# Expert loop of an attention-and-experts kernel: where the second bias is added, when GpSimd adds it, and how the routing arithmetic is spread

## The reference

```
x = x + xattn(layernorm(x), ctx)                # 16 heads, then relu(out W1 + b1) W2 + b2
logits = x @ Wg;  e = argmax(logits)            # 8 experts, one for each token
h   = gelu((xhat * s_e + b_e) @ W1_e + b1_e)    # 512 -> 128
x   = x + h @ W2_e + b2_e                       # 128 -> 512
```

## Time and profile before

| | |
|---|---|
| median of three runs | 1582.67 us |
| the profiled execution's own time | 1584.45 us |
| its span, first to last instruction | 1582.6 us |
| TensorE matmul busy | 1515.4 us, 96% |
| VectorE busy | 1037.9 us, 66% |
| ScalarE busy | 713.1 us, 45% |
| GpSimd busy | 441.9 us, 28% |
| mean granted TensorE clock | 0.987 |

### The profile page before, as it was taken

The page is one execution under the profiler, slowest core; times in us unless marked ns, Lnnn a source line. Parts: engine busy times, 40 slices in busy tenths (PEclk is TensorE's granted clock), DMA queues, the critical chain, the costliest instruction groups (busy, mean ns, idle before and its releaser), DMA issues.

```text
span 1582.6 us, 24339 instructions
## 1 busy us (share of the span) xinstructions
PE 1515.4 (96%) x7988; PEld 1254.6 (79%) x7988; DVE 1037.9 (66%) x2496; ACT 713.1 (45%) x2015; POOL 441.9 (28%) x312
## 2 busy tenths in 40 slices
PE   6799999999999999999999999999999999997998
PEld 3688788787878787878787788878787878776886
DVE  5756566675758576766666675757575757467776
ACT  2545445353535363635444353535353636333443
POOL 3422122121222222212131122122222222136776
PEclk8899999999999999999999999999999999999999
DMA  9200101112020202020101101010101011548773
GB/s 230 80 28 1 54 1 40 42 31 74 3 86 1 74 14 74 22 75 21 61 27 54 34 23 38 17 54 1 54 1 54 1 54 54 215 153 261 232 226 112
DMA packets 67736, 105.93 MB, mean 67 GB/s; under 512 B 26967, under 2 KB 35432, under 8 KB 66591
## 3 DMA queue, kind: packets, MB, share of 16 engines
q1 hardware_dynamic: 56814, 70.68, 15.9%
q0 software_dynamic: 10800, 33.70, 5.5%
HBM read 59.47 MB, written 46.72 MB: 67 GB/s over the span
## 4 chain that ended last, share of the span: by engine, by line
PE 60%; DVE 23%; DMA 7%; ACT 4%; issue 3%; POOL 2%; DVEq 0%; POOLq 0%; SPq 0%; ACTq 0%
PE bank L1025 13%; PE bank L1050 12%; PE bank L887 11%; PE bank L911 5%; PE bank L1005 5%; DMA region<-rows,pos 4%; DVE actH L994 4%; PE bank L1455 4%; PE bank L1499 4%; DMA rows<-in_x 3%; DVE xn L845 2%; POOL region L1193 2%; ACT actH L988 2%; PE bank L1119 2%; PE bank L1438 2%
## 5 line engine op out<-in xcount | busy, mean ns | idle before, releaser
L1050 PE MATMUL bank<-w,actH 128*128 128x512 f32 x1536 | 373.8, 393 | 4.6 <-DVE actH L1040 4.6
L1025 PE MATMUL bank<-actA,w 128*128 128x512 f32 x1536 | 366.7, 394 | 0.0
L1025 PEld LDWEIGHTS bank<-actA,w 128*128 128x128 f32 x1536 | 286.0, 188 | 62.2
L1050 PEld LDWEIGHTS bank<-w,actH 128*128 128x128 f32 x1536 | 282.4, 188 | 62.9 <-DVE actH L1040 8.6
L970 POOL TENSOR_TENSOR E<-E,rc 128x1232 f32<-128x1232 f32 x64 | 145.0, 2265 | 447.6 <-DVE rc L965 447.6
L1040 DVE TENSOR_TENSOR actH<-htmp,actH 128x512 fp32r<-128x512 f32 x128 | 88.7, 693 | 166.8 <-ACT actH L1036 148.1
L1035 ACT ACTIVATE htmp<-bank,b 128x512 f32<-128x512 f32 x128 | 88.2, 689 | 226.1 <-PE bank L1025 217.4
L887 PE MATMUL bank<-actA,wq 128*128 128x512 f32 x768 | 182.0, 390 | 0.0
L943 ACT ACTIVATE E<-bank,mx 128x77 f32<-128x77 f32 x512 | 157.6, 365 | 45.4 <-DVE mx L920 45.4
L887 PEld LDWEIGHTS bank<-actA,wq 128*128 128x128 f32 x768 | 144.2, 188 | 30.4 <-issue 0.5
L1193 POOL DMA_INDIRECT region<-rows,pos x64 | 63.1, 985 | 373.0 <-DVE pos L1187 333.9
(11 more groups left out here) (165 smaller groups left out, 2063.3 us busy)
## 6 DMA issues: line engine op xcount, KB each, us to landing
rowB<-region SPq DMA_DIRECT2D x71, 258.0 KB
rows<-in_x SPq DMA_DIRECT2D x64, 256.0 KB, 3.5
e_raw<-in_E SPq DMA_DIRECT2D x16, 256.0 KB, 2.7
region<-padrow SPq DMA_DIRECT2D x9, 258.0 KB, 2.6
w_raw<-in_W SPq DMA_DIRECT2D x1, 2048.0 KB, 10.3
w_raw<-in_W SPq DMA_DIRECT2D x2, 1024.0 KB, 8.5
e_parts<-e_high SPq DMA_DIRECT2D x8, 256.0 KB, 2.0
e_parts<-e_low SPq DMA_DIRECT2D x8, 256.0 KB, 2.3
```

What stands on the lines that cost most here:

```text
L1025: mm = pe.matmul(p[:], w, a, start=k == 0 and j == 0, stop=k == KD - 1 and j == 2)
L1050: mm = pe.matmul(p[:], a, w, start=m == 0 and j == 0, stop=m == MF - 1 and j == 2)
```

## The change

Four things change, all in the expert loop but for the running sum, which TABLE1 uses as well.

1. For an odd tile, the second bias is no longer added to `rowB` in B_XT. VectorE adds it in B_Y to the product, in place in PSUM, and a new step B_ROW(t), two places further in the list and after B_G(t+1), adds that sum to the row.
2. For an even tile, GpSimd's addition moves from B_XT(t+4) to a new step B_B2(t+3). It is then issued in iterations of odd t, behind the output DMA of tile t.
3. An iteration issues one tiny operation in place of two: after B_ROW's place when t is even, after B_H when t is odd. TABLE2 starts after iteration 5, SCAT comes after iteration 20, and PAD after iterations 22, 24, ... 36.
4. The running sum takes three additions of all eight columns, with distances 1, 2 and 4, over three buffers with four columns of zeros in front.

Eight registers per engine hold the experts in place of four, because an odd tile's register is now read in B_Y.

```diff
-                3: [("RK", NBLK - 1)], 5: [("COUNT", 1)], 6: [("SCAT", NBLK - 1)], 8: [("TABLE2",)]}
-        LATE.update({10 + 2 * e: [("PAD", e)] for e in range(NE)})
+                3: [("RK", NBLK - 1)], 5: [("COUNT", 1), ("TABLE2",)], 20: [("SCAT", NBLK - 1)]}
+        LATE.update({22 + 2 * e: [("PAD", e)] for e in range(NE)})
         for t in range(-5, NT):
-            for kind, ahead in (("B_Y", 0), ("B_G", 1), ("B_X", 5), ("B_XT", 4), ("B_H", 3)):
+            for kind, ahead in (("B_Y", 0), ("B_G", 1), ("B_ROW", 0), ("B_X", 5), ("B_B2", 3), ("B_XT", 4), ("B_H", 3)):
                 if 0 <= t + ahead < NT:
                     step(kind, t + ahead)
+                if kind == ("B_H" if t % 2 else "B_ROW"):
+                    step("DRIP", 1)
...
-        DRIP = {"KP": 5, "Q": 2, "PT": 2, "AV": 2, "HLO": 12, "Y": 1, "TT": 1, "B_Y": 1, "B_H": 1}
+        DRIP = {"KP": 5, "Q": 2, "PT": 2, "AV": 2, "HLO": 12, "Y": 1, "TT": 1}
...
+        def own(i, back=0):
+            return ctl[i][:, NE // 2 - back:NE // 2 - back + NE]
         def running(dve, n):
-            dve.wait_ge(dve_chain, n)
-            n = issued(dve.tensor_copy(cinc[:], ctl[:]))
-            yield
-            for e in range(1, NE):
+            for i, to in ((0, own(1)), (1, own(2)), (2, cinc[:])):
                 dve.wait_ge(dve_chain, n)
-                n = issued(dve.tensor_tensor(cinc[:, e:e + 1], cinc[:, e:e + 1], cinc[:, e - 1:e], ALU.add))
+                n = issued(dve.tensor_tensor(to, own(i), own(i, 1 << i), ALU.add))
                 yield
...
-        def add_b2(eng, who, t):
-            eng.wait_ge(S["b_xT"], t + 1)
-            if t < 2:
-                eng.wait_ge(L["eb"], 32)
+        def pool_b2(pool, t):
+            if t % 2:
+                return
+            pool.wait_ge(S["b_xT"], t + 1)
+            if t == 0:
+                pool.wait_ge(L["eb"], 32)
             r = rowB[t % NROW][:, 0:D]
-            eng.tensor_tensor(r, r, pick(b2e, expert(eng, who, t)), ALU.add).then_inc(b_xb[t % 2], 1)
+            nc.gpsimd.tensor_tensor(r, r, pick(b2e, expert(pool, "pool", t)), ALU.add).then_inc(S["b_rb"], 1)
...
         def dve_by(dve, t):
             dve.wait_ge(S["b_y"], t + 1)
-            dve.wait_ge(b_xb[t % 2], t // 2 + 1)
+            p = of("B_Y", t)
+            if t % 2:
+                dve.tensor_tensor(p[:], p[:], pick(b2e, expert(dve, "dve", t)), ALU.add).then_inc(S["b_pb"], 1)
+            else:
+                dve.wait_ge(S["b_rb"], t // 2 + 1)
+                dve_bout(dve, t)
+        def dve_brow(dve, t):
+            if t % 2:
+                dve.wait_ge(S["b_pb"], t // 2 + 1)
+                dve_bout(dve, t)
+        def dve_bout(dve, t):
             r = rowB[t % NROW][:, 0:D]
             dve.tensor_tensor(r, of("B_Y", t)[:], r, ALU.add).then_inc(S["b_out"], 1)
...
-            "B_XT": {"pe": pe_bx, "act": act_bx, "dve": dve_b2, "pool": pool_bx},
+            "B_XT": {"pe": pe_bx, "act": act_bx},
+            "B_B2": {"pool": pool_b2},
+            "B_ROW": {"dve": dve_brow},
```

More of the change, by code:

```diff
@@ L207, in xattn_moe_kernel @@
     cti = sb2("cti", [P, NE], I32)
-    ctl = sb2("ctl", [P, NE])
+    ctl = [sb2(f"ctl{i}", [P, NE // 2 + NE]) for i in range(3)]
     cinc = sb2("cinc", [P, NE])
@@ L264, in xattn_moe_kernel @@
             "pe_cnt dve_cnt dve_pad dve_tab dve_e1a pe_e1 dve_e1 act_e2 dve_e2 "
-            "b_xT b_xTs b_h b_hb b_gl b_g b_ghi b_glo b_y b_out").split()}
+            "b_xT b_xTs b_h b_hb b_gl b_g b_ghi b_glo b_y b_rb b_pb b_out").split()}
         pe_k, pe_v = S["pe_k"], S["pe_v"]
-        b_xb = [sem("b_xb0"), sem("b_xb1")]
         sched = []
@@ L1304, in chain @@
                 dve.wait_ge(L["jt"], 16)
+                for t in ctl:
+                    issued(dve.memset(t[:, 0:NE // 2], 0.0))
                 n = issued(dve.tensor_copy(cti[:], cnt[:]))
@@ L1310, in chain @@
                 dve.wait_ge(dve_chain, n)
-                n = issued(dve.tensor_copy(ctl[:], cti[:]))
+                n = issued(dve.tensor_copy(own(0), cti[:]))
                 yield
                 dve.wait_ge(dve_chain, n)
-                issued(dve.tensor_scalar(stp[:], ctl[:], -float(P), float(REG), ALU.mult, ALU.add))
+                issued(dve.tensor_scalar(stp[:], own(0), -float(P), float(REG), ALU.mult, ALU.add))
                 issued(dve.memset(don[:, NE:NE + 1], 0.0))
@@ L1338, in chain @@
                 dve.wait_ge(dve_chain, n)
-                n = issued(dve.tensor_copy(ctl[:], cti[:]))
+                n = issued(dve.tensor_copy(own(0), cti[:]))
                 yield
                 dve.wait_ge(dve_chain, n)
-                n = issued(dve.tensor_tensor(rem[:], ctl[:], don[:, 1:NE + 1], ALU.subtract))
+                n = issued(dve.tensor_tensor(rem[:], own(0), don[:, 1:NE + 1], ALU.subtract))
                 yield
@@ L1345, in chain @@
                 issued(dve.tensor_scalar(stp[:], rem[:], -float(P), float(REG), ALU.mult, ALU.add))
-                n = issued(dve.tensor_tensor(ctl[:], ctl[:], don[:, 0:NE], ALU.subtract))
+                n = issued(dve.tensor_tensor(own(0), own(0), don[:, 0:NE], ALU.subtract))
                 yield
@@ L1387, in expert @@
             return experts[who, t]
-        NREG = 4
+        NREG = 8
         def pick(ap, e):
@@ L1416, in dve_bx @@
             expert(dve, "dve", t)
-        def add_b2(eng, who, t):
-            eng.wait_ge(S["b_xT"], t + 1)
-            if t < 2:
-                eng.wait_ge(L["eb"], 32)
-            r = rowB[t % NROW][:, 0:D]
-            eng.tensor_tensor(r, r, pick(b2e, expert(eng, who, t)), ALU.add).then_inc(b_xb[t % 2], 1)
[L1426 to L1432, removed]
+        def pool_b2(pool, t):
[4 more added lines that the diff above has]
+                pool.wait_ge(L["eb"], 32)
+            r = rowB[t % NROW][:, 0:D]
+            nc.gpsimd.tensor_tensor(r, r, pick(b2e, expert(pool, "pool", t)), ALU.add).then_inc(S["b_rb"], 1)
         def pe_bx(pe, t):
```

## The result

The change made the kernel slower, by little. Its median is 1585.4 us (1583.19 to 1589.27, 8 runs) beside 1582.5 us for the kernel before (1579.81 to 1583.74, 8 runs); the ratio is 1.0023, with a 95% interval from 1.0012 to 1.0034, or 1.9 to 5.4 us. The prediction had 1576.5 us and a range up to 1583.5. The profiled executions differ by less than the medians: spans 1584.2 and 1582.6 us. What follows accounts for these two executions.

A forecast was written before the change was run, and what follows sets the result against it. TensorE was taken as the bound, gains being time it waits. Terms 4.4 + 2.6 + 0 - 3.5 + 2.9 = 6.4 us off 1584.45 gave 1578.0; with the median 1.8 lower, 1576.5 us, range 1568.5 to 1583.5.

The forecast's parts named there:

- parts 4 and 5: SCAT after iteration 20 makes VectorE wait at tile 24, 3.5 us lost; half the tile 11 pause goes, 2.9 gained.
- Part 1: Odd tile's bias in PSUM, 0.69 us an addition: pairs of iterations fall from 4.51 to 4.28-4.36 us, 4.4 us gained.
- the rival that the addition in PSUM makes it slower: Odd bias addition ahead of L1488 costs 1.21 us, pair takes 4.88, sum -11, time 1594 us; chance 0.08.
- the wait is not the addition's: Rival: L1488 stands behind something else, the pair stays 4.51 us, gain 2.0, time 1580.7 us; chance 0.08.
- Part 2: GpSimd's even-tile addition moved to three tiles ahead: slack falls from 4.8 to 1.7 us, no gain or loss booked.
- Cost nothing then: The moved GpSimd addition costs 0 in the steady state, where GpSimd has room within 4.28 us a pair.
- Part 3: Tiny routing operations, one an iteration: only even ones held by GpSimd's addition, TensorE losing about 0.5 us each; 2.6 gained.
- Nothing is held: Rival: an operation ahead of GpSimd's addition goes through in 0.14 us; gain 10.9, time 1572 us; chance 0.2.
- Together nothing: Up to iteration 9, about 1.5 us of new waits from three statistics operations cancel against old waits that go.
- SCAT takes it back: Rival: wait at tile 24 with lower clock, 5 us, and the pause does not go; 1580.7 us, chance 0.22.
- The prediction's own warning: The forecast fails most simply if VectorE's 2.9 us pause between tiles 10 and 12 turns up elsewhere.

The follow-up runs named there:

- e5: e4 with TensorE loading one register for tile 0 and using it for all tiles (right experts' weights left out): 1576.47 us, ratio 0.9958.
- e4: Kernel before with only the odd tiles' bias added in PSUM, its eight registers included: 1586.38 us, ratio 1.0014.
- e1: Changed kernel with GpSimd's addition for even tiles back at its old place, four tiles ahead: 1588.7 us, ratio 1.0023.
- e6: e2 with GpSimd's additions for even tiles up to 8 back at their old place, four tiles ahead: 1577.31 us, ratio 0.9964.
- e8: e6 with both tiny routing operations of a pair in the odd iteration, behind B_H: 1576.34 us, ratio 0.9958.
- e7: Kernel before with SCAT alone moved from after iteration 6 to after iteration 20: 1584.68 us, ratio 1.0007.
- e11: Changed kernel with all of SCAT after iteration 10 in place of 20: 1583.72 us, ratio 1.0003.
- e3: Changed kernel with PAD's eight writes eight iterations later, SCAT untouched: 1586.75 us, ratio 1.0014.
- e2: Changed kernel with SCAT's four DMAs issued one at a time, after iterations 12, 15, 18 and 21: 1581.72 us, ratio 0.9983.
- e10: e8 with TensorE's register load behind B_Y, SCAT's DMAs after iterations 6 to 12, early additions to tile 16, more early tiny operations: 1575.95 us, ratio 0.9953.

## Why the prediction was wrong, step by step

It forecast 6.4 us of gain; the profiled execution lost 1.6 us of span, the median 2.9 us. The step that failed worst is that of parts 4 and 5: it priced the place of SCAT as VectorE's wait for a late bias, and booked half of the pause at tile 11 as gained.

- **Part 1, 4.4 us: the mechanism was right, the term mis-sized.** The price in PSUM holds (0.69 taken, 0.70 measured), the pair nearly (4.28 to 4.36 forecast, mostly 4.37 measured), and so the rival that the addition in PSUM makes it slower is refuted, as is the one that the wait is not the addition's. But tiles 30 to 69 gained 2.3 us, about 0.1 a pair and not 0.2. Of what is left over twice 2.14, the prediction blamed the bias's register; e5 has that register too and runs pairs of 4.27, so this remainder goes with TensorE's own load. And the gain is not part 1's alone: alone it loses 1.6 us in that stretch (e4), because of late news from TensorE, most of which goes with TensorE's register loads (e5).
- **Part 2, nothing.** Wrong twice. "Cost nothing then" overlooked what it gives: it takes the steady part from 91.40 us (e1) to 86.20. And it overlooked what it costs: I looked for operations that would be held among the tiny ones that the change moved, and not among the others that GpSimd's moved addition would now meet, such as L1150. The last block's held operations in tiles 3 to 5 cost most of the 3.8 us (e1, e6).
- **Part 3, 2.6 us: right, but not for the first tiles.** Six operations of TABLE2 and three of the statistics are held, as counted, and behind one of TABLE2's TensorE loses about 0.5 us (e8 gives it back); the four steps gave 3.6 us. "Nothing is held" is refuted: L1276 took up to 1.70 us. The Trainium skill, "SBUF — State Buffer", section "Who interferes with whom", has the instruction issued first go first. The trace shows the exclusion, but L1150, 0.63 us ahead of the addition and held for 1.99 us, does not agree with that order. GpSimd's output DMA was already running when it started, though, as in the earlier trace rows, so it is not shown whether the addition overtook the operation or found it held. "Together nothing" for the first iterations is the step that failed here: the statistics' holds, put at 0.5 us each, and the one at L1150 made tiles 3 to 5 longer by 3.6 us together.
- **Parts 4 and 5, -3.5 and +2.9: the wrong step at the root.** I took a wait for a late bias and a pause of unknown cause for two things. They are one: the pause stands behind SCAT's four DMAs wherever these stand (tile 11 before and in e5, 25 in e7, 14 in e11, 24 after, in e1 and in e3), it does not need a late bias (e1), and it is gone when the DMAs are issued singly (e2), which leaves about 0.7 us beside most of the single ones (e8, e10). Moved, it costs 7.5 us over tiles 24 to 26 (7.06 + 4.07 + 2.79 less three times 2.14), where it had cost 5.8; the lower clock behind it is in both. The rival "SCAT takes it back" named the place and the lower clock, and its 1580.7 us was the nearest of the times given; but it too had VectorE wait for a late bias, which e1 rules out as the cause. The prediction's own warning, that the pause could turn up elsewhere, is what came.
- **The end, not in the sum at all.** GpSimd's DRAIN went from 3.23 to 5.62 us, and tile 69 to the end from 8.49 to 11.04. e7 shows that the place of SCAT does it (5.62 us), with nothing else changed. I read the chain of waits down to TensorE's last product and took the rest as fixed.

By these steps, a gain counted as plus: +1.9 for tiles 27 to 69 (95.1 to 93.2), +3.6 for the four waits, -3.8 for the first tiles, +5.8 - 7.5 for the pause (6.32 + 3.76 less twice 2.14 before), -2.5 for the end; that is -2.5, and 0.8 of the missing 0.9 is in tiles 23 to 27 of before, which were not at 2.14 either. As tiles 0 to 10 vary by over a us from one execution to another, the sum closes no better than that.

What stays open is why the chip does it. The runs show that work which TensorE has finished is taken up late while GpSimd issues indirect DMAs one behind another, by 0.8 to 1.0 us in e4 and by up to 5.5 us behind SCAT, and that VectorE's restart falls 0.03 and 0.04 us after the end of GpSimd's next addition (after, e11). In e7 the restart came 1.9 us ahead of that addition, so the addition is no full explanation. Whether it is the semaphore's increment or its reading that is held was not tried.

## What to carry to other kernels

When an instruction is moved in time, list what it will run beside at its new place, the untouched instructions above all; where two engines hold each other up, every move can be a swap of partners. A long unexplained wait should be tied to the instruction it stands behind before it is booked as gained: moving that instruction alone, in the kernel before (e7), would have shown at once that the pause and the end move with it. In this kernel four indirect DMAs in a row on GpSimd did better issued one at a time between other work (e2, 6.3 us); look at the end of the kernel too, to the last DRAIN.

## What the hardware showed that I had not expected

- GpSimd's closing DRAIN took 3.23 us with SCAT after iteration 6 (3.31 in e5), 3.50 after 10, 3.72 with single DMAs after 6 to 12, and 5.62 with SCAT after 20 or singly after 12 to 21. The place of SCAT sets it (e7), over a hundred microseconds before the end; PAD's later writes do not (e3 has 5.62 as well). Why is open.
- VectorE's whole addition in place in PSUM (128x512, other input in SBUF) took 699 ns, as much as from PSUM to SBUF, and was never held by GpSimd (677 to 700 ns in 35 times).
- TensorE's load of a register from SBUF, 308 ns at the median, took up to 930 ns (e4). In e8, 43 of its 44 loads over 0.45 us overlap an issue of GpSimd's, and 15 of the 27 shorter ones.
- With one register load in place of 71, the same kernel was 8.9 us faster (e5 against e4). It leaves out the right experts' weights, so it shows what the loads cost and is not a kernel to use.
